# Softplus of the next half ahead of the messages, and one PE signal per half for edges and for filters, in a graph kernel's convolution

## The reference

```python
# layer 1: two rounds of batch norm, relu, linear to 5 types x 128, gather msg = h3[src, etype],
#          segment sum over dst; then x = layernorm(x + ...)
# layer 2 (continuous-filter convolution):
h = x @ W_in
W_ij = (softplus(f_ij @ Wf1 + bf1) - log 2) @ Wf2 + bf2      # f_ij: 32 values an edge
W_ij = W_ij * f_ij_cutoff
x_ij = h[idx_j] * W_ij                                       # idx_j = destination of the sorted list
out = segment_sum(x_ij, idx_i)                               # idx_i = source
return ssp(out @ Wo1 + bo1) @ Wo2 + bo2                      # then x = layernorm(x + ...)
```

## Time and profile before

| | |
|---|---|
| median of 3 runs | 8408.23 us (8375.33 to 8417.95) |
| the profiled execution | 8335.65 us, its span in the trace 8333.8 us |
| plain steps, in the trace | 5026 to 6567 us |
| summing steps, in the trace | 6588 to 7951 us |
| busiest engines over the span | POOL 56%, PE 54%, DVE 43%, PEld 41%, ACT 16% |
| granted clock of PE, mean | 0.713 of full speed |

### The profile page before, as it was taken

How to read it: one execution, slowest core, us unless ns; L and a number is a source line. 1 busy time by engine, 2 the same in 40 slices (tenths; PEclk the granted TensorE clock), 3 DMA queues, 4 the chain that set the end, 5 groups by cost and what they waited for, 6 DMA issues and landing times.

```text
span 8333.8 us, 89560 instructions
## 1 busy us (share of the span) xinstructions
PE 4465.5 (54%) x21555; PEld 3450.3 (41%) x21555; DVE 3576.1 (43%) x7435; ACT 1301.6 (16%) x3301; POOL 4693.9 (56%) x4809
## 2 busy tenths in 40 slices
PE   5233232323345444444545556666677676676787
PEld 3222222222233333333333334555555565565676
DVE  6222222222244444444445554333333455555577
ACT  2000000000011000000000004444444333333303
POOL 3666666666644666666665555665665544444413
PEclk8555556556667777777777877666666778878799
DMA  6111111111133111111112222222222344444476
GB/s 230 46 44 44 46 44 45 44 45 45 45 103 117 43 42 43 42 43 44 43 43 64 71 70 82 82 82 83 82 82 83 109 137 136 136 138 135 140 245 212
DMA packets 406720, 710.67 MB, mean 85 GB/s; under 512 B 103887, under 2 KB 180850, under 8 KB 405940
## 3 DMA queue, kind: packets, MB, share of 16 engines
q1 hardware_dynamic: 255766, 387.96, 14.9%
q0 software_dynamic: 150912, 322.24, 13.5%
HBM read 509.88 MB, written 199.90 MB: 85 GB/s over the span
## 4 chain that ended last, share of the span: by engine, by line
another core or an unknown queue 35%; PE 26%; issue 18%; DVE 15%; DVEq 3%; ACT 2%; POOL 1%; SPq 1%; DMA 0%; ACTq 0%; POOLq 0%
PE banks L1467 6%; PE banks L1363 6%; PE banks L1456 3%; DVE work L818 3%; PE banks L1512 3%; PE banks L1340 2%; PE banks L1324 2%; DVE biased L1187 2%; DVE first_place L830 1%; PE banks L1481 1%; DVE work L828 1%; DVE work L1083 1%; DVE work L833 1%; PE banks L1339 1%
## 5 line engine op out<-in xcount | busy, mean ns | idle before, releaser
L506 POOL DMA_INDIRECT edge_rows<-messages,idx_stage x1568 | 1498.1, 955 | 1060.0 <-issue 574.3
L550 POOL DMA_INDIRECT sorted_rows<-edge_rows,idx_stage x784 | 799.5, 1020 | 717.4 <-DVE edge_rows L1191 497.9
L550 POOL DMA_INDIRECT sorted_rows<-buf_a,idx_stage x784 | 793.4, 1012 | 652.5 <-DVE buf_a L1191 417.3
L506 POOL DMA_INDIRECT buf_a<-messages,idx_stage x784 | 748.4, 955 | 464.2 <-issue 234.1
L506 POOL DMA_INDIRECT buf_x<-messages,idx_stage x784 | 748.1, 954 | 412.0 <-issue 238.0
L1467 PE MATMUL banks<-work,buf_a 128*128 128x128 f32 x4744 | 723.6, 310 | 456.2 <-DVE buf_x L1149 294.8
L1363 PE MATMUL banks<-onehot,edge_rows 128*128 128x128 f32 x3136 | 572.6, 345 | 724.3 <-DVE buf_a L904 369.1
L1363 PEld LDWEIGHTS banks<-onehot,edge_rows 128*128 128x128 f32 x3136 | 545.9, 256 | 849.7 <-issue 446.9
L1467 PEld LDWEIGHTS banks<-work,buf_a 128*128 128x128 f32 x4744 | 663.5, 221 | 550.0 <-DVE buf_x L1149 326.5
L1339 PE MATMUL banks<-work,ones_b 128*128 128x392 bf16 x392 | 166.4, 424 | 1197.7 <-DVE first_place L830 640.8
L1363 PE MATMUL banks<-onehot,buf_x 128*128 128x128 f32 x1568 | 321.2, 378 | 879.6 <-DVE buf_a L904 566.2
(11 more groups left out here) (165 smaller groups left out, 6562.2 us busy)
## 6 DMA issues: line engine op xcount, KB each, us to landing
buf_a<-sorted_rows SPq DMA_DIRECT2D x593, 288.0 KB
messages<-work SPq DMA_DIRECT2D x196, 320.0 KB, 2.2
buf_a<-dst_rows SPq DMA_DIRECT2D x198, 256.0 KB
buf_a<-in_attr SPq DMA_DIRECT2D x198, 128.0 KB
buf_a<-h_in SPq DMA_DIRECT2D x396, 64.0 KB
edge_rows<-messages,idx_stage POOLq DMA_INDIRECT x1568
buf_x<-messages,idx_stage POOLq DMA_INDIRECT x784
buf_a<-messages,idx_stage POOLq DMA_INDIRECT x784
```

What stands on the lines that cost most here:

```text
L506: nc.gpsimd.indirect_dma_start(gathered[p][h][:, t, :], None, source, bass.IndirectOffsetOnAxis(ap=idx_stage[:, h, t:t + 1], axis=0),).the ...
L550: nc.gpsimd.indirect_dma_start(sorted_rows, bass.IndirectOffsetOnAxis(ap=idx_stage[:, 2 * u + h, t:t + 1], axis=0), msg_halves[2 * u + h][ ...
```

## The change

The softplus of half `k + 1` is made ahead of the messages of half `k`. For that ACT's order becomes softplus of `k + 1`, copies of `k`; DVE's `soft_half(k + 1)` stands before the messages of `k` and writes to one of two buffers (`soft_halves`); PE's `filter_in` of `k + 1` stands before the edges of `k`. Ln now writes in place of Abs (`abs_z`), which frees `log_z` for the second buffer. `s_hexp` and `s_w` are raised once for a half, after both groups, and their waiters count halves. DVE stages the cutoff of `k + 1` once the copies of `k - 1` are done, and waits for the copy of each group just before it multiplies.

```diff
@@ -188,6 +188,7 @@
         out_rows = work[:, 0:SLOTS * TD].rearrange("p (q n) -> p q n", q=SLOTS)
         stage5 = work[:, :].rearrange("p (a j n) -> p a j n", a=5, j=2)
         abs_z, relu_z, log_z, soft = (stage5[:, a] for a in range(4))
+        soft_halves = [stage5[:, 3], stage5[:, 2]]
         high_hot = work[:, SLOTS * TD:SLOTS * TD + 2 * HOT].bitcast(bf16).rearrange("p (h j n) -> p h j n", h=2, j=2)
         picked = work[:, SLOTS * TD + 2 * HOT:SLOTS * TD + 3 * HOT]
         place_stage = work[:, SLOTS * TD + 3 * HOT:SLOTS * TD + 3 * HOT + 2 * HALF_TILES].rearrange("p (h t) -> p h t", h=2)
@@ -429,7 +430,7 @@
                         load_attributes(h, k + 2)
                         sp.wait_ge(s_spread, k * 2 + 2)
                         load_ends(h, k + 2)
-                        sp.wait_ge(s_hexp, k * 2 + 2)
+                        sp.wait_ge(s_hexp, k + 1)
                         load_windows(h, bases[2 * h:2 * h + 2])
 
                 with sp.Fori(0, FIRST_ITERS + 1) as r:
@@ -616,24 +617,22 @@
 
                 for j in range(2):
                     act.wait_ge(s_z, k * 2 + (j + 1))
-                    act.wait_ge(s_act, k * 6 + 1)
+                    act.wait_ge(s_soft, k * 2 + (j + 1))
                     nc.scalar.activation(abs_z[:, j, :], ps_z[j], ACT.Abs).then_inc(s_act, 1)
                 for j in range(2):
                     act.wait_ge(s_act, k * 6 + (2 + j))
                     nc.scalar.activation(abs_z[:, j, :], abs_z[:, j, :], ACT.Exp, scale=-1.0).then_inc(s_act, 1)
                 for j in range(2):
                     act.wait_ge(s_act, k * 6 + (4 + j))
-
-                    act.wait_ge(s_soft, k * 2 + SLOT2)
-                    nc.scalar.activation(log_z[:, j, :], abs_z[:, j, :], ACT.Ln, bias=half_col[:, 0:1],
+                    nc.scalar.activation(abs_z[:, j, :], abs_z[:, j, :], ACT.Ln, bias=half_col[:, 0:1],
                                          scale=0.5).then_inc(s_act, 1)
 
             def convolution_step(r):
                 for h in range(2):
                     k = r * 2 + h
+                    softplus_half(k + 1)
+                    act.wait_ge(s_hexp, k + 1)
                     for j in range(2):
-
-                        act.wait_ge(s_hexp, k * 2 + (j + 1))
                         act.wait_ge(s_msg, k * 2 + (j + 1))
                         act.wait_ge(s_cut, k + 4)
                         for t in range(GROUP_TILES):
@@ -641,7 +640,6 @@
                             last = nc.scalar.activation(h_edge[:, j, tile], ps_h[j][:, tile], ACT.Copy,
                                                         scale=cut_stage[:, h, i:i + 1])
                         last.then_inc(s_hcopy, 1)
-                    softplus_half(k + 1)
 
 
             nc.scalar.add_instruction(mybir.InstLoadActFuncSet(
@@ -1076,12 +1074,12 @@
             first_places()
             round_pass(1)
 
-            def soft_half(k):
+            def soft_half(k, h):
                 for j in range(2):
 
                     dve.wait_ge(s_act, k * 6 + (6 + j))
-                    nc.vector.scalar_tensor_tensor(out=soft[:, j, :], in0=ps_z[j], scalar=0.0,
-                                                   in1=log_z[:, j, :], op0=ALU.max, op1=ALU.add).then_inc(s_soft, 1)
+                    nc.vector.scalar_tensor_tensor(out=soft_halves[h][:, j, :], in0=ps_z[j], scalar=0.0,
+                                                   in1=abs_z[:, j, :], op0=ALU.max, op1=ALU.add).then_inc(s_soft, 1)
 
             def spread_half(it, h):
 
@@ -1165,7 +1163,7 @@
                     spread_half(r + h, 1 - h)
                     if adding:
                         add_step(0)
-                    dve.wait_ge(s_hcopy, k * 2 + (2 + SLOT2))
+                    dve.wait_ge(s_hcopy, k * 2 + ((2 + SLOT2) if beyond else SLOT2))
                     stage_cutoff(r + h, 1 - h)
                     if adding:
                         add_step(1)
@@ -1179,8 +1177,9 @@
                     stage_indices(2, k, 2 * u + h)
                     nc.vector.tensor_copy(messages[:, :, D],
                                           src_idx[:, ds(r * ITER_TILES + h * HALF_TILES, HALF_TILES)]).then_inc(s_tagged, 1)
+                    soft_half(k + 1, 1 - h)
+                    dve.wait_ge(s_w, k + 1)
                     for j in range(2):
-                        dve.wait_ge(s_w, k * 2 + (j + 1))
                         dve.wait_ge(s_msg, k * 2 + (j + SLOT2))
                         tiles = "p (t n) -> p t n"
                         in_tiles = biased.rearrange(tiles, t=GROUP_TILES)
@@ -1188,12 +1187,12 @@
                                                 filter_bias[:, :].unsqueeze(1).broadcast_to([P, GROUP_TILES, D]),
                                                 ALU.add).then_inc(s_biased, 1)
                         dve.wait_ge(s_biased, k * 2 + (j + 1))
+                        dve.wait_ge(s_hcopy, k * 2 + (j + 1 + SLOT2))
                         nc.vector.tensor_tensor(messages[:, j * GROUP_TILES:(j + 1) * GROUP_TILES, 0:D], in_tiles,
                                                 h_edge[:, j, :].rearrange(tiles, t=GROUP_TILES), ALU.mult
                                                 ).then_inc(s_msg, 1)
                         if adding:
                             add_step(2 + j)
-                    soft_half(k + 1)
 
             scale_rows(CHUNKS_IN - 1)
             dve.wait_ge(s_acc[1], GROUPS + SLOT2)
@@ -1205,7 +1204,7 @@
             for c in (edge_rows, buf_a[:, MSG_COLS:MSG_COLS + 2 * HALF_TILES * ROW]):
                 nc.vector.memset(c.rearrange("p (t n) -> p t n", n=ROW)[:, :, D:ROW], 0.0).then_inc(s_cut, 1)
             scale_rows(CHUNKS_IN)
-            soft_half(0)
+            soft_half(0, 0)
             dve.wait_ge(s_cut, 4)
             dve.wait_ge(s_placed_out, 2 * ITERS + SLOT2)
             dve.wait_ge(s_zeroed, CHUNKS)
@@ -1471,6 +1470,10 @@
             def convolution_step(r, beyond, adding):
                 for h in range(2):
                     k = r * 2 + h
+                    filter_in(k + 1, 1 - h, (r + h) * 16 + 16)
+                    if adding:
+                        turn = r - (FIRST_ITERS + 1)
+                        sum_segment(turn * STEP_SLOTS + 4 * h, 4 * h, 0)
                     for j in range(2):
 
                         pe.wait_ge(s_win_in[h], r * 32 + 32)
@@ -1480,11 +1483,7 @@
                             tile = slice(t * P, (t + 1) * P)
                             last = nc.tensor.matmul(ps_h[j][:, tile], spread[:, h, j * WIDE + t * P:j * WIDE + (t + 1) * P],
                                                     h_win[:, h, j, :], start=True, stop=True)
-                        last.then_inc(s_hexp, 1)
-                    if adding:
-                        turn = r - (FIRST_ITERS + 1)
-                        sum_segment(turn * STEP_SLOTS + 4 * h, 4 * h, 0)
-                    filter_in(k + 1, 1 - h, (r + h) * 16 + 16)
+                    last.then_inc(s_hexp, 1)
                     if adding:
                         sum_segment(turn * STEP_SLOTS + (4 * h + 1), 4 * h + 1, 0)
                     if beyond:
@@ -1509,10 +1508,11 @@
                         if beyond:
                             pe.wait_ge(s_xadd, (k * 2 + 2) * BLOCKS + 1)
                         for t in range(GROUP_TILES):
-                            last = nc.tensor.matmul(ps_w[j][:, t * D:(t + 1) * D], soft[:, j, t * P:(t + 1) * P],
+                            last = nc.tensor.matmul(ps_w[j][:, t * D:(t + 1) * D], soft_halves[h][:, j, t * P:(t + 1) * P],
                                                     wf2[:, :], start=True, stop=True)
-                        last.then_inc(s_w, 1)
-                        if adding:
+                    last.then_inc(s_w, 1)
+                    if adding:
+                        for j in range(2):
                             sum_segment(turn * STEP_SLOTS + (4 * h + 2 + j), 4 * h + 2 + j, 0)
 
             def convolution(beyond):
```

## The result

The changed kernel takes 8322.94 us (median of 4 runs, 8318.21 to 8334.28), the kernel before beside it 8413.09 us (8375.33 to 8425.49). The medians are 90 us apart. The ratio by which runs are compared here is 0.9905, 95% interval 0.9876 to 0.9934: faster by about 1%, 56 to 104 us. The forecast was 8442 us and slower.

The account below looks back on a forecast made before the run. PE's completion signals, late while POOL issues scatter DMAs, were taken to bound each half. Plain -85 us and summing +119 us gave +34 on the median of 8408, so 8442 us, range 8270 to 8590.

Parts of the forecast that it names:

- The plain term: Plain steps: softplus ahead of messages shortens the tail behind late signals, 1.5 us for each of 57 pairs, -85 us.
- 13.5 falls to 12.8: Plain steps: the time for a half would fall from 13.5 to 12.8 us, a sign of the forecast.
- One reading: Single signal for edges, plain steps: both groups' signals land together at the run's end, so it costs nothing.
- One sign: Plain steps: ACT's Abs starts inside POOL's run; a start after the run would mean Rival 2.
- The summing term: Summing steps: one more filter group ahead of the filters' signal, 1.45 us x 82 halves, +119 us.
- The price of a group: Summing steps: eight more filter matmuls L1512 on the path, taken as 1.45 us, between 0.95 and 1.9.
- Rival 1: Both stages: fewer PE signals let late ones through; 8315 us, or 8252 with longer POOL runs; chance 0.32.
- Rival 2: Plain steps: softplus ahead of ACT's copies delays the message, +1.9 us x 57, +106; 8633 us; chance 0.15.
- Rival 3: Both stages: late PE signals end each half alike, so pieces swap one for one; 8380 to 8430 us; chance 0.15.

Follow-up runs that it names:

- run 10: Kernel before with one signal for a half for the edges alone, signals on time: 6669 us against 6671, ratio 0.9997.
- run 11: Kernel before with one signal for a half for the filters alone, signals on time: 6731 us against 6671, ratio 1.0094.
- run 14: Kernel before with one signal for a half for edges and one for filters, signals late: 8195 us against 8189, ratio 1.0008.
- run 2: Changed kernel with the signals of before (each group, a sum between filter groups), signals on time: 7175 us against 6671 for the kernel before.
- run 1: Changed kernel, nothing else altered, where signals are on time: 7148 us against 6671 for the kernel before, ratio 1.0711.
- run 15: Changed kernel with the signals of before (each group, a sum between filter groups), signals late: 8221 us against 8189 for the kernel before.
- Runs 4: Changed kernel with two more signals in each half that nobody waits for, signals on time: 7151 us against 6671 for the kernel before.
- Run 13: Changed kernel with sorted rows loaded ahead of the edges' wait and eight unused matmuls per summing half, signals late: 8127 us against 8189 before.
- runs 7 and 17: Kernel before, unchanged, single executions for a trace: 6649 us where signals are on time, 8336 us where they are late.

## Why the prediction was wrong

**The plain term, nearly right.** I took -85 us from the tail behind the late signals (2.64 us before, 0.9 to 1.3 forecast). It is 0.8 us in the shown pair, and the stage gave 73 us there and 68 us on chip 6. "13.5 falls to 12.8" came out as 12.87. Part of that is luck: of the 73 us only 47 are POOL's waits for messages (379.4 to 331.9 us), the tail's share; about 18 more lie in POOL's own busy time (928.12 to 909.93 us), which the prediction didn't have. One reading was wrong: the prediction has both signals of the edges landing together at the run's end, while its own rows have the copies start at 6005.47 and 6009.66; with one signal for both, where nothing is late, run 10 costs nothing. One sign failed: ACT's Abs did not start inside POOL's run but at its end with all others, 5679.87. It costs nothing in this pair, because PE is one half further: the copies of this half are done (their signal came through during the run), and the message waits for the filters' signal alone.

**The summing term, wrong: this is the step that failed.** "In the summing steps it costs. There PE's order puts the filters behind segment sum 4h+1, and that one behind DVE's addition of sum 4h, whose signal is late", so one more group of filters, "1.45 us x 82 halves: +119 us". Measured: +17 and +18 us in the two pairs of traces. With that in place of +119 my sum would have been -68 us, inside the 56 to 104 us that were measured. The price of a group was nearly right where signals are on time: 0.88 us with the clock at its upper level (run 11). Where they are late, run 14 has the path that I described and costs 6 us in all, so the 119 us are not shown there either. And in the changed kernel the path is gone; the order alone, without that group, is no shorter (run 2, 16.06 us for a half against 15.69). Here are the waits of DVE's addition in the summing steps, for the changed kernel also those of its one-hot and bias, in the kernel before and then in the changed one (us in total, times, longest):

```profile
DVE buf_x L1149 <- remote: 441.6, 89, 6.9
...
DVE buf_x L1149 <- PE banks L1467: 94.4, 68, 2.5
```

```profile
DVE buf_x L1147 <- PE banks L1466: 355.6, 132, 4.9
...
DVE buf_x L1147 <- remote: 82.7, 17, 6.3
DVE work L1132 <- DMA buf_a<-sorted_rows: 76.8, 79, 2.6
...
DVE biased L1186 <- PE banks L1511: 0.9, 1, 0.9
```

441.6 - 82.7 = 359 us of waiting for late signals went, and waits for PE's recorded work and for the sorted rows came in their place. DVE's bias, which stands behind the filters, waits for them once, 0.9 us (87.8 us in 96 waits before): the filters now run beside DVE's softplus. I had it the other way, the softplus hidden behind the filters. The chain of waits of the changed kernel over one summing half reads:

```profile
7001.53 3.65 PE banks L1484 x16
...
7007.57 2.81 DMA buf_a<-sorted_rows
...
7011.52 1.89 PE banks L1466 x8
7013.41 3.71 PE banks L1455 x4
7017.11 2.00 PE banks L1466 x8
7019.12 3.22 PE banks L1484 x16
```

This is the loop of run 1, with the same pieces, 17.6 us round. It is not in every half. SP's waits for the edges, ahead of its windows, read in these steps:

```profile
SPq L383 <- PE banks L1484: 738.4, 64, 11.9
SPq L383 <- remote: 209.8, 17, 13.3
```

64 end with PE's recorded work, as in the loop, and 17 with a late signal. I priced each moved step by what stood behind it on its own engine, but didn't follow SP's queue from the edges' signal to the sorted rows, which DVE needs in the same half. One bound of 16.7 us was exchanged for another, mostly this loop, of 16.9. That the two are so close is chance: with signals on time the first is 10.1 and the second 15.7.

**Rival 1** has the right sign and nearly the right time (8315), and half its mechanism: the addition of sum 4h is no longer late. But the cause that it gives, fewer signals, is not what does it in the summing steps: run 14 has fewer signals and the waits, run 15 has the old number and hardly any. Runs 4 and 10, where nothing is late, can't tell. For the plain steps the two are not separated, 12.62 us for the order alone and 12.73 for the signals alone. By the Trainium skill's 26.3 ns for a completion increment (TensorE: Matmul & The Clock Gate, "The cost: per-tile semaphore tail") the edges' 196 would have given 5 us less as an estimate; run 10 measured 2 us less, with an interval from 8 less to 4 more, and so neither bears that out nor excludes it. **Rival 2** did not come, although Abs starts after the run: the message of the shown pair doesn't wait for the copies, and over the whole span the messages wait for them 7.6 us. **Rival 3**, pieces that swap one for one, is what the summing steps did by another mechanism.

**Not settled.** The two trace pairs put 55 and 57 us on the convolution, less 5 or 6 behind it, and chip 6 measures 38 us. The first comparison measures 90 (56 to 104). What is missing may lie in the rounds ahead, whose code is the same: the first message comes anywhere from 5006 to 5076 us in eight traces with late signals. On chip 11 order alone and signals alone give nothing, although their plain halves are 12.6 and 12.7; a trace of the kernel before is missing there. Taking a first message at 5006 to 5021 us and 387 to 390 us behind the last, as in the three traces of that chip, off its 8189 us leaves some 2780 to 2790 us for its convolution, an estimate, where chip 6 had 2895. So its halves seem to be short there already, and the gain in the plain steps is shown in the first pair and on chip 6 only. Why signals are late on some chips, and why PE's new order has fewer of them in the summing steps, no run shows. Run 13, where PE is faster and they are back, suggests that they come when PE signals early in POOL's run.

## What to carry over

When a producer's step moves later on its engine, follow its signal through every queue that it releases, DMA queues too, to the next wait of the same loop: here one load of rows queued behind a load of windows closed a loop of 16 us. Time a change to a kernel whose bound is a late signal on more than one chip: this one is 0.5 to 1% faster where signals are late and 7% slower where they are on time. Where PE waits a little in each turn of a loop, look at the granted clock before its matmuls are counted.

## What the runs showed of the hardware

The same kernel takes 6655 to 6671 us on four chips, 8189 and 8319 us on two others, and 8413 us in the first comparison. The traces differ in PE's completion signals while POOL issues indirect DMAs back to back: nothing is late on the four, and on the others signals land late, in the shown pairs the last of them 3.2 and 3.5 us after POOL's last start. Of the 1687 us between the two traces of the kernel before (runs 7 and 17), 811 lie ahead of the first message (4242 against 5053 us) and 878 in the convolution (2017 against 2895 us). Eight unused matmuls in each summing half made the changed kernel 281 us faster, with the clock from 0.74 to 0.96.
